# Attention layers 1 and 2 in even steps: each unit's scores ahead of its transposes by three units, GpSimd folding and multiplying the probabilities, layer 2 clamping the row maximum

## The reference, cut to what matters

```python
# layer 1 (8 heads of 16), after layer norms
Q = (lat @ W_Q).reshape(B, Lq, H, dqk); K = (inp @ W_K)...; V = (inp @ W_V)...
attn = softmax(einsum('bqhd,bkhd->bhqk', Q, K) * scale, axis=-1)
out  = einsum('bhqk,bkhd->bqhd', attn, V).reshape(B, Lq, V_CH) @ W_O
# layer 2 (16 heads of 8), with biases
attn = einsum('bhqd,bhkd->bhqk', q, k) * scale
attn = softmax(clip(attn, -CLAMP, CLAMP), axis=-1)
x    = einsum('bhqk,bhkd->bqhd', attn, v).reshape(B, Nq, Cq) @ Wo + bo
# each is added to the stream with a gate
x = x + tanh(g_xattn[l]) * attention_l(layernorm(x), ctx)
```

## Time and profile before

| | us |
|---|---|
| median of 3 runs | 1289.16 |
| lowest, highest | 1282.66, 1290.75 |
| profiled execution | 1284.38 |
| its span, first to last instruction | 1282.5 |

### The profile page before, as it was taken

The page is one execution under the profiler, slowest core; times in us unless marked ns, Lnnn a source line. Parts: engine busy times, 40 slices in busy tenths (PEclk is TensorE's granted clock), DMA queues, the critical chain, the costliest instruction groups (busy, mean ns, idle before and its releaser), DMA issues.

```text
span 1282.5 us, 23078 instructions
## 1 busy us (share of the span) xinstructions
PE 897.3 (70%) x7875; PEld 717.9 (56%) x7876; DVE 797.4 (62%) x1904; ACT 476.5 (37%) x1085; POOL 233.3 (18%) x280
## 2 busy tenths in 40 slices
PE   0336444069974983889875779983899999729892
PEld 0215221056753872656653679982678777628771
DVE  3866878957874226887867546546666566562334
ACT  1441327134551551344441433331343434205551
POOL 1000000000001660000000047750000000017771
PEclk9758676578995995586775789995899999759996
DMA  8200000014001118000000111118000000011113
GB/s 199 73 1 1 1 1 0 0 62 87 0 1 40 46 48 229 1 0 0 0 1 1 33 32 47 47 40 214 1 2 0 0 0 0 2 38 48 49 51 111
DMA packets 73144, 48.27 MB, mean 38 GB/s; under 512 B 19642, under 2 KB 65732, under 8 KB 73092
## 3 DMA queue, kind: packets, MB, share of 16 engines
q1 hardware_dynamic: 64484, 31.80, 9.3%
q0 software_dynamic: 6656, 13.64, 3.6%
q10 hardware_dynamic: 1952, 2.15, 0.6%
HBM read 33.93 MB, written 13.63 MB: 37 GB/s over the span
## 4 chain that ended last, share of the span: by engine, by line
PE 47%; DVE 27%; POOL 9%; issue 7%; ACT 5%; DMA 2%; DVEq 0%; SPq 0%; POOLq 0%; ACTq 0%
PE ps L1914 6%; POOL rows_y L499 5%; POOL arena L494 4%; PE ps L1747 4%; PE ps L1778 3%; PE ps L1928 3%; PE ps L1808 3%; PE ps L1503 3%; PE ps L1767 3%; PE ps L1704 3%; PE ps L1714 2%; PE ps L1792 2%; PE ps L1731 2%; PE ps L1756 2%; DVE bst L523 2%
## 5 line engine op out<-in xcount | busy, mean ns | idle before, releaser
L1914 PE MATMUL ps<-arena 128*128 128x128 f32 x1152 | 153.3, 283 | 0.0
L494 POOL DMA_INDIRECT arena<-rows_x,row_in x104 | 102.5, 985 | 275.9 <-DVEq L1116 245.1
L1914 PEld LDWEIGHTS ps<-arena 128*128 128x128 f32 x1152 | 141.0, 197 | 1.5
L499 POOL DMA_INDIRECT rows_y<-arena,row_out x104 | 109.4, 1052 | 55.3 <-issue 21.0
L1928 PE MATMUL ps<-arena 128*128 x832 | 115.5, 282 | 1.2 <-DVE arena L1079 1.1
L1066 DVE COPY arena<-arena 128x644 f32 (+1 forms) x104 | 62.0, 596 | 78.6 <-DVE arena L1079 32.1
L1928 PEld LDWEIGHTS ps<-arena 128*128 128x128 f32 x832 | 101.0, 191 | 5.9 <-issue 2.8
L1503 PE MATMUL ps<-ident,xh 128*128 128x128 f32 x128 | 37.1, 445 | 85.7 <-DVE xh L555 69.7
L1314 ACT ACTIVATE arena<-arena 128x512 f32<-128x512 f32 (+1 forms) x96 | 53.7, 559 | 111.6 <-DVE arena L838 111.3
L1440 ACT ACTIVATE arena<-ps,arena 128x128 f32<-128x128 f32 x256 | 73.0, 367 | 46.7 <-PE ps L1914 46.7
L846 DVE TENSOR_REDUCE arena<-arena 128x8 f32<-128x512 f32 (+1 forms) x96 | 57.1, 594 | 44.8 <-ACT arena L1314 43.5
(11 more groups left out here) (289 smaller groups left out, 1753.9 us busy)
## 6 DMA issues: line engine op xcount, KB each, us to landing
arena<-rows_y SPq DMA_DIRECT2D x20, 256.0 KB, 4.7
arena<-in_L_ffn_w SPq DMA_DIRECT2D x2, 2048.0 KB, 9.3
arena<-in_L_ffn_w SPq DMA_DIRECT2D x16, 256.0 KB, 6.6
rows_x<-xh SPq DMA_DIRECT2D x3, 1024.0 KB, 5.1
rows_x<-zero SPq DMA_DIRECT2D x1, 2560.0 KB, 10.2
arena<-in_L_ffn_gate_proj SPq DMA_DIRECT2D x8, 256.0 KB, 5.1
arena<-in_L_ffn_up_proj SPq DMA_DIRECT2D x8, 256.0 KB, 5.2
arena<-in_L_ffn_down_proj SPq DMA_DIRECT2D x1, 2048.0 KB, 10.7
```

The source lines that it names most:

```text
L494: g.indirect_dma_start(xq[:, q % 4, :], None, rows_x, bass.IndirectOffsetOnAxis(row_in[:, q:q + 1], 0)).then_inc(sem(f"xq_loaded{q % 4}"), 16)
L499: g.indirect_dma_start(rows_y, bass.IndirectOffsetOnAxis(row_out[:, q:q + 1], 0), yq[:, q % 4, :], None).then_inc(sem(f"y_scattered{q % 4} ...
L1914: ins = pe.matmul(ps[:, 2 * m + s_ % 2, P * f:P * f + P], wst[:, s_ % 4, lo:lo + P], xqT[:, s_ % 2, :], start=True, stop=True)
```

## The change

PE's steady order for layers 1 and 2 becomes four steps per group. Steps 0 to 2 are: scores u of this group, turn u+1 of the group before, values u+1 of the group before. Step 3 is: value rows, scores 3, turn 0 of this group, queries and keys of the next group, project the group before, values 0. The three filler matmuls now follow each turn, in both layers, and eight of them stand in each of the three empty places of the first group; the 30 are gone. After the last group three units of turns and values follow.

The row sum is split: GpSimd adds the two halves of each 64-column row (`total`), DVE sums the 32 columns that are left and takes the reciprocal (`inverse`), and GpSimd multiplies (`weigh`). In layer 2 the full-width clamp is replaced by a clamp of the maximum, a combined lower clamp and subtraction straight from PSUM, and a `min` with 0 in place in SBUF. `values` alternates the halves `hh` and writes the second to PSUM partitions 64 to 127, and `narrow` is four copies of 32 x 64. Keys go to bank 6 beside the queries, the projection goes to bank 7.

```diff
+            def weigh_groups(l, src):                      # GpSimd
+                def total(i, u):
+                    g.wait_ge(sem("s_exp"), UNITS * i + (UB[l] + u + 1))
+                    p_ = t["p"][:, u, 0:w].rearrange("p (n s) -> p n s", s=S)
+                    g.tensor_tensor(t["half"][:, u, 0:n, :], p_[:, :, 0:S // 2], p_[:, :, S // 2:S], ALU.add
+                                    ).then_inc(sem("half_ready"), 1)
+                def weigh(i, u):
+                    g.wait_ge(sem("rec_ready"), UNITS * i + (UB[l] + u + 1))
+                    g.tensor_tensor(p_, p_, t["rec"][:, u, 0:n].unsqueeze(2).to_broadcast([P, n, S]), ALU.mult
+                                    ).then_inc(sem("prob"), 1)
+                def group(i, first=False):
+                    stage_context(i)
+                    if not first:
+                        weigh(i - 1, 3)
+                    total(i, 0)
+                    for u in range(1, UNITS):
+                        weigh(i, u - 1)
+                        total(i, u)
...
+                    own(v.tensor_reduce(t["max"][:, u, 0:n], s_, AX.X, ALU.max))      # DVE scores
+                    own.wait()
+                    top = t["max"][:, u, 0:n].unsqueeze(2).to_broadcast([P, n, S])
                     if l == 2:
-                        own(v.tensor_scalar(p_, s_, CLAMP, -CLAMP, ALU.min, ALU.max))
+                        own(v.tensor_scalar(t["max"][:, u, 0:n], t["max"][:, u, 0:n], CLAMP, -CLAMP, ALU.min, ALU.max))
                         own.wait()
+                        own(v.scalar_tensor_tensor(p_, s_, -CLAMP, top, ALU.max, ALU.subtract))
+                        own.wait()
+                        own(v.tensor_scalar(p_, p_, 0.0, None, ALU.min), f"s_sub_{l}")
+                        return
+                    own(v.tensor_tensor(p_, s_, top, ALU.subtract), f"s_sub_{l}")
+                def inverse(i, u):
+                    v.wait_ge(sem("half_ready"), UNITS * i + (UB[l] + u + 1))
+                    own(v.tensor_reduce(t["sum"][:, u, 0:n], t["half"][:, u, 0:n, :], AX.X, ALU.add))
+                    own.wait()
+                    v.reciprocal(t["rec"][:, u, 0:n], t["sum"][:, u, 0:n]).then_inc(sem("rec_ready"), 1)
...
+                        scores(i, 0)                       # DVE group, layers 1 and 2
+                        if not first:
+                            inverse(i - 1, 3)
+                        scores(i, 1)
+                        inverse(i, 0)
+                        if first and l == 2:
+                            add_offset()
+                        scores(i, 2)
+                        inverse(i, 1)
+                        scores(i, 3)
+                        if more:
+                            keys(i + 1)
+                        inverse(i, 2)
+                        if not first:
+                            add_group(i - 1)
...
+                    for u in range(3):                     # ACT group
+                        if not first:
+                            probT(i - 1, u + 1)
+                        expo(i, u)
+                        if not first:
+                            narrow(i - 1, u + 1)
                     values(i)
                     probT(i, 0)
                     if more:
                         queries(i + 1)
                     expo(i, 3)
+                    narrow(i, 0)
...
-                    for c in range(2):                     # ACT narrow
-                        ins = s.copy(t["o"][32 * u:32 * u + 32, 0:GT]...[:, :, c, :], ps[32 * c:32 * c + 32, 4 + u % 2, 0:P]...)
+                    for b in range(4):
+                        ins = s.copy(t["o"][32 * u:32 * u + 32, S * b:S * b + S], ps[32 * b:32 * b + 32, 4 + u % 2, 0:S])
...
-                    if l == 1:                             # PE turn
-                        dense(2 + u % 2, 30 if isinstance(i, int) and i == u == 0 else 3)
                     pe.wait_ge(sem("prob"), UNITS * i + (UB[l] + u + 1))
                     for k in range(sub):
                         ins = pe.transpose(ps[:, 2 + u % 2, P * k:P * k + P], t["p"][:, u, P * k:P * k + P], ident[:, :])
                     ins.then_inc(sem("pT_mm"), 1)
+                    if l != 3:
+                        dense(3 - u % 2, 3)
...
-                        for hh in range(2):                # PE values
-                            for k in range(sub):
-                                ins = pe.matmul(ps[0:64, 4 + u % 2, S * hh:S * hh + S],
+                        for k in range(sub):
+                            for hh in range(2):
+                                ins = pe.matmul(ps[64 * hh:64 * hh + 64, 4 + u % 2, 0:S],
...
+                    if l != 3:                             # PE group
+                        for u in range(3):
+                            scores(i, u)
+                            if not first:
+                                turn(i - 1, u + 1)
+                            if first:
+                                dense(3, 8)
+                            else:
+                                values(i - 1, u + 1)
+                        value_rows(i)
+                        scores(i, 3)
+                        turn(i, 0)
+                        if more:
+                            queries_keys(i + 1)
+                        if not first:
+                            project_out(i - 1)
+                        pe.wait_ge(sem(f"v_ready_{l}"), i + 1)
+                        values(i, 0)
+                        return
...
+                if l != 3:                                 # PE, after the last group
+                    for u in range(1, UNITS):
+                        turn(NG - 1, u)
+                        values(NG - 1, u)
```

More of the change, by code:

```diff
@@ L889, in group @@
                 def group(i, first=False, more=True):
-                    weigh(i, 1)
-                    scores(i, 2)
-                    if not first:
-                        add_group(i - 1)
-                    weigh(i, 2)
-                    scores(i, 3)
-                    if more:
-                        keys(i + 1)
-                    weigh(i, 3)
-                    if l == 3:
-                        outputs(i, 0)
-                    if more:
-                        scores(i + 1, 0)
-                        weigh(i + 1, 0)
-                        scores(i + 1, 1)
@@ L907, in group @@
-                    if l == 3:
+                    if l != 3:
[14 more added lines that the diff above has]
+                            add_group(i - 1)
+                    else:
+                        weigh(i, 1)
+                        scores(i, 2)
+                        if not first:
+                            add_group(i - 1)
+                        weigh(i, 2)
+                        scores(i, 3)
+                        if more:
+                            keys(i + 1)
+                        weigh(i, 3)
+                        outputs(i, 0)
+                        if more:
+                            scores(i + 1, 0)
+                            weigh(i + 1, 0)
+                            scores(i + 1, 1)
@@ L927, in attention @@
                 keys(0)
-                scores(0, 0)
-                weigh(0, 0)
-                scores(0, 1)
-                if l > 1:
-                    own.wait()
-                    own(v.tensor_tensor(x[:, :, :], x[:, :, :], offset[:, :].unsqueeze(1).to_broadcast([P, NT, P]), ALU.add))
-                    own.wait()
+                if l == 3:
+                    scores(0, 0)
+                    weigh(0, 0)
+                    scores(0, 1)
+                    add_offset()
                 group(0, first=True)
@@ L1367, in narrow, with group @@
                     s.wait_ge(sem(f"av_mm_{l}"), UNITS * i + (u + 1))
[L1368 to L1370 removed]
+                    for b in range(4):
+                        ins = s.copy(t["o"][32 * u:32 * u + 32, S * b:S * b + S], ps[32 * b:32 * b + 32, 4 + u % 2, 0:S])
                     ins.then_inc(sem(f"o_other_{l}"), 1)
[L1373 to L1374 removed]
+                def group(i, more, first=False):
+                    if l == 3:
+                        values(i)
                         expo(i, 1)
+                        probT(i, 0)
+                        expo(i, 2)
+                        probT(i, 1)
+                        if more:
+                            queries(i + 1)
+                        expo(i, 3)
+                        probT(i, 2)
+                        outputs(i, 0)
+                        if more:
+                            expo(i + 1, 0)
+                        probT(i, 3)
+                        outputs(i, 1)
+                        return
[5 more added lines that the diff above has]
+                            narrow(i - 1, u + 1)
                     values(i)
[L1377 to L1378 removed]
                     probT(i, 0)
[L1380 to L1382 removed]
                     if more:
@@ L1402, in attention @@
                 queries(0)
```

(14 more changed lines are left out.)

89 lines of the change are left out of this document (46 added, 43 removed).

## The result

The change made the kernel 1.1% slower, where the forecast was 1261 us, which would be 2.2% faster.

A forecast was written before the change was run, and what follows sets the result against it. PE was taken as nearly the bound in layer 1; in layer 2 DVE's chain alternated with PE at 1.2 GHz. Layer 1 -3.5 and layer 2 -24 took 1284.4 to 1257; medians lie 4.8 higher: 1261 us, range 1244 to 1284.

The forecast's parts named there:

- The clock is taken as full: Layer 2: PE's remaining idle pieces, 0.5 us a step and 1 us a group, were taken to leave full clock.
- the low clock: Rival, layer 2 stays at 1.2 GHz, about 19.5 us a group: 1286 us (chance 0.06), or half the time, 1268 (0.08).
- the loop through GpSimd: Rival, both layers: inverse, product and fold become a slower loop, groups 13.9 and about 21.3 us, 1323 us; chance 0.08.
- Its argument against: Against a low clock in layer 2: layer 1 holds full clock with the same fillers.
- Layer 1, -3.5 us: Layer 1's attention: a group takes 9.9 us against 10.42, six times -0.5, and the tail 14.4 against 14.9.
- called the narrow copies hidden: Layer 2: narrow copies cost ACT 1.2 us a group, hidden since ACT is busy 68 of 165 us.
- The layer's two ends: Layer 1: the fill stays, about 14 us either way; the tail of three units takes 14.4 us against 14.9.
- Layer 2, -24 us: Layer 2's attention: a group takes 16.3 us against 19.7, six times -3.4 is -20.4; tail 22.3 against 26.
- DVE's wait for the shared ports: Layer 2: DVE blocked by GpSimd, +0.5 us a unit; as a rival, 1286 us (chance 0.09) or about 1271 (0.09).
- the forecast second level: Layer 2, DVE's `min`: two levels of time should show, 0.42 and over 1 us.
- The estimate of 1.2 us for the wide product: GpSimd's 512-column product by the skill's 4497 ns for 2048 elements; the loop would be about 2.9 us.
- Values by alternating halves: PE's values blocks take about half the time: 0.33 us for 0.61 in layer 1, 0.62 for 1.07 in layer 2.

The follow-up runs named there:

- first experiment: Changed kernel with six fillers after each turn instead of three, and eight more at the end of step 3, in layers 1 and 2; 1261.84 us, ratio 0.9752.
- fifth experiment: Changed kernel with `values` and `narrow` as in the old kernel (one half after the other, two copies of 32 x 128); 1268.59 us, ratio 0.9816.
- seventh experiment: Changed kernel with its three fillers after each turn, and eight more only in step 3 ahead of the wait for the keys; 1271.87 us, ratio 0.9843.
- the mixed version: Layer 1 as in the old kernel; layer 2 as changed, with six fillers after each turn and eight ahead of the keys' wait; 1252.66 us, ratio 0.9699.
- the ninth: Layer 1 as in the old kernel; layer 2 as changed, with three fillers after each turn and eight more in step 3; 1258.41 us, ratio 0.9746.
- eleventh experiment: The old kernel without layer 1's filler matmuls; 1320.29 us, ratio 1.0251.

## Why the prediction was wrong

**The step that failed** is "The clock is taken as full: the idle pieces left are 0.5 us a step and 1 us a group, where the falls stood behind 2 us." The sizes of the idle pieces were about right: the waits for ACT are 0.4 to 1.0 us a step, and the one for the keys 1.1. PE in the changed kernel's full-clock group of layer 2 (the scores' starts bound the group):

```profile
606.75 1.08 PE L1831 MATMUL ps<-arena 32*64 32x256 f32 x8 [1.13 <-DVE arena L909]
...
609.17 0.69 PE L1862 MATMUL ps<-arena 128*64 128x64 f32 x16 [0.43 <-ACT arena L1388]
...
612.80 0.69 PE L1862 MATMUL ps<-arena 128*64 128x64 f32 x16 [1.03 <-ACT arena L1388]
...
615.83 0.69 PE L1862 MATMUL ps<-arena 128*64 128x64 f32 x16 [0.42 <-ACT arena L1388]
```

What they do was wrong. I had read from one fall that it takes one long gap. The clock falls with none as long as 1 us, and then stays low for more than a group. That the low clock is the loss is shown by the first and fifth experiments, and by the seventh in layer 2. Which property of PE's work lets it fall is shown only in part: filler and a longer values block hold it, but the idle share alone doesn't order the cases. With the clock held by filler the program takes 1261.84 us, the number of the forecast. That is luck, since it comes by other terms: layer 1 is 12 us longer than forecast, layer 2 3 us shorter, the part ahead of layer 1, with the early start, is 5 us shorter and stood in no term, and the rest is 3 us longer.

**The rival that came true** was the low clock, given 0.06 and 0.08 and confined to layer 2. Even it put the time at 1286 us; all of the 0.08 for a slower kernel was given to the loop through GpSimd, which didn't come. Its argument against, that layer 1 holds full clock with the same fillers, took layer 1's clock for a property of its fillers. But it hung on the rest of PE's work too: layer 1 had PE busy 95% of the time, and the change removed work there, 0.9 us a group. No rival had the clock fall in layer 1, where the largest loss is. The low clock was also priced too low: 19.5 us for a layer-2 group wholly at 1.2 GHz, against 21.8 at a mean of 0.58.

**Layer 1, -3.5 us.** Wrong at full clock too: 10.7 us a group against 9.9 forecast and 10.42 before. Steps 0 and 2 take 1.87 us from scores to scores against 1.81; step 1 takes 2.64. The cause is ACT:

```profile
330.95 0.42 ACT L1384 ACTIVATE arena<-arena 128x256 f32<-128x256 f32 x1 [0.96 <-DVE arena L881]
331.39 0.85 ACT L1438 COPY arena<-ps 32x64 f32<-32x64 f32 x4
332.27 0.37 ACT L1388 COPY arena<-ps 128x256 f32<-128x256 f32 x1
```

The exponential waits for DVE; the four narrow copies (0.85 us) and the transposed probabilities (L1388) stand behind it in ACT's order; PE's values at 332.69 wait 0.92 us. With the two copies of the fifth experiment (0.52 us) that wait is 0.35 us. The prediction called the narrow copies hidden because ACT's share was low. That holds for its busy time, not for the copy that is queued behind them. The keys cost 0.35 to 0.64 us of waiting, as put. The layer's two ends were sized wrong as well: with the clock held, layer 1 is 8.3 us longer than the old one, of which five groups explain 3.6. The old first group ran 30 fillers in one block. In the new one the fillers stand in three places, and the clock rises later; that the one is the reason for the other isn't tested. Windows of the first experiment's trace, its layer 1 beginning at 281.75, and below them one of the kernel before, its layer 1 beginning at 286.68:

```profile
288.00:295.00 7.00, 7.00 (x40) 4.67 (x40) 2.53 (x8) 0.91 (x3) 2.49 (x5) 0.50 1.03 207
295.00:302.00 7.00, 6.90 (x52) 5.02 (x50) 2.81 (x8) 2.79 (x10) 1.00 (x3) 0.75 0.15 1
...
297.00:302.00 5.00, 4.49 (x41) 3.36 (x38) 1.87 (x5) 1.95 (x7) 0.00 (x0) 1.00 0.62 50
```

Thirteen us into the layer the clock is still at 1.2 GHz; in the old kernel it is full 10 us into the layer.

**Layer 2, -24 us.** Right while the clock holds: 15.4 us against 16.3 put; stage 141.6 us in the first experiment against 144.9. DVE's wait for the shared ports is there, but far smaller than the 2 us a group that were put. Of the layer's 32 clamps of eight columns 26 take 0.17 us and six take 0.35 to 0.55, until the end of a GpSimd product, fold or copy that ran beside them. All 32 `min` take 0.43 us, so the forecast second level never came; none of them ran beside a GpSimd instruction, so this trace doesn't show what one would have cost. The Trainium skill (SBUF — State Buffer, Who interferes with whom) has one of the two engines blocked for a whole instruction of the other; the longer clamps agree. But part of the 24 us belonged to the clock, not to the order: the old order with enough filler gains 8.1 us of the stage by itself (168.9 to 160.8).

**GpSimd.** Product 0.61 and 1.04 us (0.62 and 1.06 put), fold 0.45 and 0.72 (0.40 and 0.62 put). One product of the layer's first group took 2.97 us. The estimate of 1.2 us for the wide product, made in the prediction from the Trainium skill (GPSIMD Engine Reference, Elementwise), is above the 1.04 us measured; in plain proportion the page's figure gives 1.12. The rival of a loop through GpSimd is refuted: the part is worth 1.5 us a layer-2 group and 0.6 in layer 1.

**Values by alternating halves.** Start to start 0.38 us in layer 1 and 0.62 in layer 2, against 0.33 and 0.62 put and 0.61 and 1.07 before. The size was right, the sign of its effect wrong: with this part and its narrow copies taken back, the program is faster.

## What to carry to other kernels

When a change shortens PE's own work or moves a wait next to it, first add up PE's idle time in a full-clock group and compare it with a stretch of the same trace that holds the clock. If it grew, count the low clock among the rivals, with a price read from a low-clock stretch. Then put filler where the waits are, and change the amount in both directions in the first experiments; the sum of idle time doesn't tell beforehand how much is needed. Judge each layer by itself at the same clock: here one order was better in layer 2 and worse in layer 1, and the mixed version beat both kernels by 3.0 and 4.0% in ratio (5.5 us of the gain over the old kernel lie ahead of layer 1, with the early start). Compare kernels stage by stage as well, since a change can move time in code that it doesn't touch. A share of busy time doesn't make an engine's work hidden; what counts is the instruction queued behind it.

## What the runs showed of the hardware

- The granted clock fell with no wait of PE as long as 1 us in the 16 us before (changed kernel, layer 1, 328.56 to 344.62 us); the group there had PE idle 17%. With 7% idle in layer 2 (first experiment) and 10% in layer 1 (fifth) it stayed, but with 7% in layer 1 (seventh) it fell. With 13% in layer 2 it stayed in the seventh experiment, and the same code lost it in the ninth. What decides between them is open.
- The granted clock stayed at half while PE had no idle time in the profile: 27.0 us at 0.51 (changed kernel, from 301 us) and 29.7 us at 0.50 (eleventh experiment, from 340 us).
- DVE's clamp of eight columns took 0.17 us, and 0.35 to 0.55 in six cases beside a GpSimd instruction (changed kernel, layer 2).
- In the eight kernels with two-input operations of GpSimd in the attention, GpSimd's 10 us of idle time at the start of the program is gone (0.3 us); the other six have it.
- Eight 64-column matmul pairs that alternate between the PSUM halves take 0.62 us start to start where the same in one half took 1.07.
- GpSimd's two-input float32 operations took 0.61 us for 256 columns and 1.04 for 512.
